# A two-layer graph network on one core: the transpose of h moved from TensorE to a DRAM scratch, block loads and VectorE, with the layer norm of x one stage earlier

## What is computed

```python
# layer 0
h = maximum(layernorm(x), 0)
q, k, v = h @ Wq.T + bq, h @ Wk.T + bk, h @ Wv.T + bv
weight = adj * exp(q @ k.T)
x = x + (weight / sum(weight, axis=2)) @ v
# layer 1
h = maximum(layernorm(x), 0)
A_hat = adj + eye;  d = A_hat.sum(-1) ** -0.5
x = x + (A_hat * d[:, :, None] * d[:, None, :]) @ (h @ W + b)
```

## Time and profile before

| | |
|---|---|
| three runs, us | 1748.71, 1750.32, 1751.24 (median 1750.32) |
| the profiled execution, us | 1750.99, its span 1749.1 |
| PE busy | 1725.3 us, 99% of the span |
| DVE, ACT, POOL busy | 1266.5, 746.5, 555.7 us |
| mean granted clock of TensorE | 0.997 of full speed |
| DMA moved | 105.55 MB, mean 60 GB/s |

### The profile page before, as it was taken

One profiled execution on the slowest core, in us unless ns is written; L12 is line 12 of the kernel. 1 busy time (PEld: TensorE's weight loads), 2 busy tenths in 40 slices (PEclk: granted clock), 3 DMA queues, 4 the chain that ended last, 5 costly groups with the idle time before them and its releaser, 6 DMA issues.

```text
span 1749.1 us, 32667 instructions
## 1 busy us (share of the span) xinstructions
PE 1725.3 (99%) x11452; PEld 1574.7 (90%) x11452; DVE 1266.5 (72%) x3097; ACT 746.5 (43%) x1546; POOL 555.7 (32%) x585
## 2 busy tenths in 40 slices
PE   7999999999999999999999999999999999999997
PEld 5899999999999999999999999999999999999996
DVE  5677777777777777777767777777777777777774
ACT  3444344353444444444443443534444444434432
POOL 1323323323323323333233233233233233332331
PEclk9999999999999999999999999999999999999999
DMA  5212212212122122122122121121221221221210
GB/s 157 61 43 66 69 39 72 60 48 72 54 54 72 54 54 72 48 60 71 41 68 67 41 72 55 53 72 54 54 72 51 57 72 43 65 69 39 72 48 25
DMA packets 191978, 105.55 MB, mean 60 GB/s; under 512 B 140512, under 2 KB 156896, under 8 KB 191968
## 3 DMA queue, kind: packets, MB, share of 16 engines
q1 hardware_dynamic: 190048, 103.84, 21.0%
q10 hardware_dynamic: 1920, 1.58, 0.3%
HBM read 71.83 MB, written 33.55 MB: 60 GB/s over the span
## 4 chain that ended last, share of the span: by engine, by line
PE 98%; DVE 1%; issue 0%; ACT 0%; DMA 0%; POOL 0%; ACTq 0%; POOLq 0%; DVEq 0%
PE ps L546 31%; PE ps L548 31%; PE ps L547 31%; PE ps L630 3%; PE ps L556 1%; PE ps L613 1%; DMA late<-in_L_gnn_Wq_w_dram 0%; ACT late L287 0%; DVE p_lo L515 0%; ACT h_hi L289 0%; DVE z_lo L486 0%; DVE late L492 0%; DVE w_in L395 0%; DVE wvt_lo L385 0%; POOL hat_lo L227 0%
## 5 line engine op out<-in xcount | busy, mean ns | idle before, releaser
L287 ACT ACTIVATE late<-late,nb,sc 128x512 f32<-128x512 f32 x128 | 103.6, 809 | 587.5 <-DVE nb L443 587.5
L546 PE MATMUL ps<-ht_hi,m_hi 128*128 128x256 f32 x1024 | 287.3, 281 | 0.8 <-DVE wvt_lo L385 0.8
L547 PE MATMUL ps<-ht_lo,m_hi 128*128 128x256 f32 x1024 | 288.0, 281 | 0.0
L548 PE MATMUL ps<-ht_hi,m_lo 128*128 128x256 f32 x1024 | 287.5, 281 | 0.0
L224 POOL TENSOR_TENSOR hat_hi<-adjt,eye 128x512 fp32r<-128x512 f32 x64 | 82.7, 1293 | 580.4 <-DVE p_lo L515 580.4
L546 PE MATMUL ps<-w_hi,z_hi 128*128 128x512 f32 x512 | 207.7, 406 | 1.5 <-DVE z_lo L486 1.5
L548 PE MATMUL ps<-w_hi,z_lo 128*128 128x512 f32 x512 | 202.4, 395 | 0.0
L547 PE MATMUL ps<-w_lo,z_hi 128*128 128x512 f32 x512 | 202.3, 395 | 0.0
L546 PE MATMUL ps<-wvt_hi,ht_hi 128*128 128x512 f32 x512 | 202.2, 395 | 0.0
L548 PE MATMUL ps<-wvt_hi,ht_lo 128*128 128x512 f32 x512 | 202.1, 395 | 0.0
L547 PE MATMUL ps<-wvt_lo,ht_hi 128*128 128x512 f32 x512 | 202.0, 395 | 0.0
(11 more groups left out here) (102 smaller groups left out, 4529.1 us busy)
## 6 DMA issues: line engine op xcount, KB each, us to landing
x_in<-in_x_dram SPq DMA_DIRECT2D x64, 512.0 KB, 3.5
out_dram<-late SPq DMA_DIRECT2D x128, 256.0 KB, 2.0
adj_in<-in_adj_dram SPq DMA_DIRECT2D x64, 256.0 KB, 2.8
adj_blocks<-in_adj_dram SPq DMA_DIRECT2D x256, 64.0 KB, 2.8
late<-in_L_gnn_Wk_w_dram SPq DMA_DIRECT2D x4, 256.0 KB, 4.9
late<-in_L_gnn_Wq_w_dram ACTq DMA_DIRECT2D x4, 256.0 KB, 7.7
wv_in<-in_L_gnn_Wv_w_dram SPq DMA_DIRECT2D x1, 1024.0 KB, 7.9
w_in<-in_L_gnn_W_dram SPq DMA_DIRECT2D x1, 1024.0 KB, 7.7
```

What stands on the lines that cost most here:

```text
L287: act.activation(h1[:, t, :], x1[:, t, :], ACT.Relu, scale=sc_1[:, t:t + 1], bias=nb_1[:, t:t + 1])
L546: pe.matmul(dst, a_hi[:, c, cols], b_hi[:, c, :], start=(c == 0), stop=False)
L547: pe.matmul(dst, a_hi[:, c, cols], b_lo[:, c, :], start=False, stop=False)
L548: last = pe.matmul(dst, a_lo[:, c, cols], b_hi[:, c, :], start=False, stop=(c == chunks - 1))
```

## The change

In all steps but the first, `h` is no longer transposed by PE. SP stores `h` to a DRAM scratch (`h_scratch`), waits for the store, and loads it back with four DMAs as 32x32 blocks (`load_h_blocks`); VectorE transposes the blocks with two instructions (`transpose_h`) to `ht` in SBUF; `ht_hi` and `ht_lo` are then made from `ht` where they were made from PSUM. So that `h` is there early enough, ScalarE makes `h` of the next graph as the first thing of a step instead of in the middle, and VectorE takes the statistics of x two graphs ahead. `x_in` is then free before the residual is needed, so x is loaded a second time, into `xb`, after `x1` of the graph before has been read, and GpSimd adds `bv` in place, later in its order. GpSimd also waits for `ht_lo` before it makes `hat`.

```diff
+        def load_h_blocks(sp):
+            rows = h_dram.rearrange("(g r) (c q j) -> q r c g j", r=32, c=DC, q=P // 32, j=32)
+            for q in range(P // 32):
+                sp.dma_start(h_blocks[q * 32:(q + 1) * 32].rearrange("r c (g j) -> r c g j", j=32),
+                             rows[q]).then_inc(h_blocks_loaded, 16)
...
             sp.dma_start(x_in[:], x[0].rearrange("(t p) d -> p t d", p=P)).then_inc(x_loaded, 16)
+            sp.dma_start(xb[:], x[0].rearrange("(t p) d -> p t d", p=P)).then_inc(xb_loaded, 16)
...
                     sp.dma_start(adj_in[:], adj_next.rearrange("(t p n) -> p t n", p=P, n=N)).then_inc(adj_loaded, 16)
+
+                    sp.wait_ge(h_ready[0], this + 1)
+                    sp.wait_ge(h_ready[1], this + 1)
+                    if prev:
+                        sp.wait_ge(h_blocks_loaded, (this - 1) * (16 * P // 32))
+                    sp.dma_start(h_dram.rearrange("(t p) d -> p t d", p=P), h[:]).then_inc(h_stored, 16)
+                if second:
+                    x_second = x_flat[bass.ds(sp.snap((this + 1) * (N * D)), N * D)]
...
+                    sp.dma_start(x_in[:], x_second.rearrange("(t p d) -> p t d", p=P, d=D)).then_inc(x_loaded, 16)
+                if main and prev:
...
+                    sp.wait_ge(x1_ready[0], this - 1)
+                    sp.wait_ge(x1_ready[1], this - 1)
+                    sp.dma_start(xb[:], x_this.rearrange("(t p d) -> p t d", p=P, d=D)).then_inc(xb_loaded, 16)
                 if main and ahead:
-                    sp.wait_ge(h_ready[1], this)
-                    sp.wait_ge(xb_ready, this)
-                    sp.dma_start(x_in[:], x_next.rearrange("(t p d) -> p t d", p=P, d=D)).then_inc(x_loaded, 16)
-                if main and ahead:
+                    sp.wait_ge(h_stored, this * 16)
+                    if prev:
+                        sp.wait_ge(ht_ready[1], this - 1)
+                    load_h_blocks(sp)
                     sp.wait_ge(adjt_ready, this)
                     load_blocks(sp, adj_next)
...
                     pool.wait_ge(p_lo_ready[1], this - 1)
+                    if main:
+                        pool.wait_ge(ht_lo_ready[1], this)
...
+                    pool.wait_ge(xb_loaded, this * 16)
+                    for t in range(NT):
+                        last = pool.tensor_tensor(xb[:, t, :], xb[:, t, :], bv_row[:], ALU.add)
+                    last.then_inc(xb_ready, 1)
...
+            def layer_norm_x(this, prev):
+
+                act.wait_ge(ln_x_ready, this + 1)
+                if prev:
+                    act.wait_ge(h_stored, (this - 1) * 16)
+                for t in range(NT):
+                    if prev:
+                        act.wait_ge(vk_ready[t], this)
+                    act.activation(h[:, t, :], x_in[:, t, :], ACT.Relu, scale=rs_x[:, t:t + 1],
+                                   bias=nb_x[:, t:t + 1]).then_inc(h_ready[t], 1)
...
+            def transpose_h(this, prev):
+
+                dve.wait_ge(h_blocks_loaded, this * (16 * P // 32))
+                for j in range(2):
+                    dve.wait_ge(ht_hi_ready[j], this)
+                    dve.wait_ge(ht_lo_ready[j], this)
+                    dve.transpose(ht[:, 2 * j:2 * j + 2, :].rearrange("p c n -> p (c n)"),
+                                  h_blocks[:, 2 * j:2 * j + 2, :].rearrange("p c n -> p (c n)")).then_inc(ht_ready[j], 1)
...
                     for c in range(DC):
-                        if prev and c % 2 == 0:
-                            pe.wait_ge(z_lo_ready[c // 2], this - 1)
                         for t in range(NT):
                             last = pe.transpose(ps[:, HT + c // 2, c % 2 * N + t * P:c % 2 * N + (t + 1) * P],
```

More of the change, by code:

```diff
@@ L162, in steps @@
             step(2, prev=True, main=True, ahead=True, older=False)
-            with eng.Fori(3, B) as this:
+            with eng.Fori(3, B - 1) as this:
                 step(this, prev=True, main=True, ahead=True)
-            step(B, prev=True, main=True, ahead=False)
-            step(B + 1, prev=True, main=False, ahead=False)
+            step(B - 1, prev=True, main=True, ahead=True, second=False)
+            step(B, prev=True, main=True, ahead=False, second=False)
+            step(B + 1, prev=True, main=False, ahead=False, second=False)
         @block.sync
@@ L215, in _, with step @@
             pool.wait_ge(ident_ready, 2)
-            def step(this, prev, main, ahead, older=True):
+            def step(this, prev, main, ahead, older=True, second=True):
                 if prev:
@@ L227, in step @@
                     pool.tensor_tensor(hat_lo[:], hat[:], hat_hi[:].bitcast(fp32), ALU.subtract).then_inc(hat_lo_ready, 1)
[L228 to L238, removed]
                     pool.wait_ge(ve_1_done, this - 1)
@@ L280, in value_high, with step @@
                 act.activation(v_hi[:, t, :, 0:HD], halves(ps[:, V + t, :]), ACT.Copy).then_inc(v_hi_ready[t], 1)
-            def step(this, prev, main, ahead, older=True):
+            def layer_norm_x(this, prev):
[7 more added lines that the diff above has]
+                                   bias=nb_x[:, t:t + 1]).then_inc(h_ready[t], 1)
+            def step(this, prev, main, ahead, older=True, second=True):
+                if main and ahead:
+                    layer_norm_x(this, prev)
                 if prev:
@@ L302, in step @@
                     value_high(1, this)
[L303 to L309, removed]
+                if ahead and not main:
+                    layer_norm_x(this, prev)
+                    m_high()
                 if prev:
@@ L458, in step @@
                         last.then_inc(g_lo_ready[j], 1)
[L459 to L479, removed]
+                if ahead and not main:
+                    statistics(this + 1)
+                    m_low()
+                if second and main:
+                    statistics(this + 2, lambda: value_low(0, this), lambda: value_low(1, this))
                 elif main:
@@ L482, in step @@
                     value_low(1, this)
+                if main and ahead:
+                    transpose_h(this, prev)
                 if prev:
@@ L527, in step @@
                         score_bias(this + 1)
+                        statistics(this + 2)
                 if prev:
@@ L576, in bias_and_wv_products, with step @@
                 pe.wait_ge(wvt_lo_ready, 2)
-            def step(this, prev, main, ahead, older=True):
+            def step(this, prev, main, ahead, older=True, second=True):
                 if main:
+                    pe.wait_ge(ht_lo_ready[0], this)
                     pe.wait_ge(ht_lo_ready[1], this)
@@ L619, in step @@
                                 (g_hi, g_lo), cols, (ht_hi, ht_lo)).then_inc(s_done[t], 1)
[L620 to L623, removed]
+                if ahead and not main:
+                    m_product()
+                    pe.wait_ge(ident_ready, 1)
                     pe.wait_ge(h_ready[0], this + 1)
```

59 lines of the change are left out of this document (47 added, 12 removed).

## The result

The changed kernel takes 1703.34 us (median of 4, 1702.79 to 1703.71) against 1750.65 us for the kernel before beside it (4 runs, 1748.71 to 1751.24). The ratio is 0.9731, 95% interval 0.9715 to 0.9748. Predicted were 1704, faster, in 1697 to 1735. The profiled execution took 1703.36 us, span 1701.6.

The account below looks back on a forecast made before the run. PE was taken as the bound, busy for all 26.58 us of a step. 1751.0 - 54.6 (transposes) + 8.0 (start-up) = 1704.4 us, 1703.7 for the median; forecast 1704, own range 1700 to 1708, stated range 1697 to 1735.

Parts of the forecast that it names:

- 0.88 us a step for the transposes on PE: Between S and O1 on PE, removing eight transposes saves 0.88 us in each of 62 steps, 54.6 us.
- DVE's 1.42 us are hidden: Two block transposes on DVE between nb_x and z_lo fit its idle time; z_lo keeps 1.0 to 1.6 us before O1.
- The start-up, +8 (4.9 to 9.9): In step 1, O waits for h's store, loads and transposes ahead of p, beginning 4.9 to 9.9 us later; 8 taken.
- Block loads land 10.6 us after G starts (8.1 to 13.1): Last block load of h lands at 911.0 to 916.0, middle 913.5, before DVE's turn at 915.8; PE loses nothing.
- Rival 1: Blocks of h land late, DVE stands ahead of z_lo, kernel slower; landing at 919.5 gives 1834 us; 11%.
- Rival 2, POOL and DVE block each other: POOL's xb add falls beside DVE's h_lo; held by one add 1704 to 1720 us, by both 1760; 16%.
- `hat` behind `ht_lo`: nothing: POOL's hat starts 1.2 us later, takes 3 x 1.3 us, needed by Z 11.3 us after G starts: no cost.
- DMA share 0.45: The DMA engines' share of a step rises from 0.20 to some 0.45, as 1.5 MB a step become 3.
- Layer norm ahead: ACT makes the next graph's h at the step's start; the forecast sum counts no gain for this.

Follow-up runs that it names:

- experiment 1: Changed kernel with PE's eight transposes of h put back between S and O1, their result read by nobody: 1757.94 us, 1.0043 of the kernel before.
- experiment 8: Changed kernel with DVE, in step 1 alone, making graph 3's statistics and the transposes of h behind p_lo: 1697.31 us, 0.9706 of the kernel before.
- Experiment 7: Changed kernel in which POOL's hat no longer waits for ht_lo: 1711.79 us (median of three), 0.9776 of the kernel before.
- experiment 2: Changed kernel with only the earlier layer norm and second x load; PE transposes h as before, no scratch or block loads: 1753.95 us, 1.0022 of the kernel before.
- experiments 9 to 11: POOL makes rs_x ahead of the xb add, added to the kernels with two more DVE transposes, four more, and hat not waiting for ht_lo: 1711.87, 1784.45, 1709.92 us.
- experiment 4: Changed kernel with four more DVE block transposes behind the wait for the block loads, from step 2 on: 1797.49 us, 1.0269 of the kernel before.

## Why the prediction was right, point by point

The forecast was 1704.4 for the profiled execution, which took 1703.36. The loop gave 54.1 us where 54.6 were foretold, and the start-up cost 6.8 where 8 was taken out of a range of 5 us. That the sum came within 1.1 us is the mechanism for the loop, and in part luck for the start-up.

- *0.88 us a step for the transposes on PE*: 0.35 us between the two starts as foretold; the step went from 26.57 to 25.70, 0.87. Shown by experiment 1, which puts it back.
- *DVE's 1.42 us are hidden*: 1.30 us, hidden; 1.57 us remain to O1 in the step shown (1.0 to 1.6 foretold). But the prediction priced this slack in one undisturbed step. `nb_x` is up to 1.49 us late in others, and what is left there is 0.2 us. That no step of the loop lost time was closer than the working knew, and so partly luck.
- *The start-up, +8 (4.9 to 9.9)*: 6.8. O begins at 54.97, inside 53.1 to 58.1. It is due to DVE's order, since experiment 8 takes it away. By the terms, `h` stood at 40.2 (39.4 foretold), the store landed at 43.4 (42.9), the last block at 49.9 (47.9 to 52.9). The working left out that the statistics of the third x stand ahead of the transposes and wait 2.48 us for their load; they were done at 48.4, ahead of the blocks.
- *Block loads land 10.6 us after G starts (8.1 to 13.1)*: too early. In steps 3 to 62 of after the last one lands at 12.25 in the median, from 10.7 to 14.0. The store lands at 3.8 (3.1 foretold); from the first issue to the last it is 4.9 us (2.2 to 4.4 foretold), and that term is the one that was mis-sized; from the last issue to the landing 3.6 (2.8 to 5.6). DVE's turn is at 12.8, and by the slack of 1.69 PE loses from some 14.5 on. For the loads of x the 3.5 us of the earlier trace rows did not hold either: each step sends 1.5 MB more through the same queue, and they land in 6.6 and 7.6 us. Rival 1 was nearer than its 11% looked: two more loads cost some 38 us, 1741.21 against 1703.34.
- *Rival 2, POOL and DVE block each other*: happened, at another instruction than the one named, and inside the slack. `h_lo` has 727 ns in the mean and is held in 3 cases of 122 between 80 and 1650 us, up to 1.78 us. The `xb` add was expected at 908 to 913, 5 to 10 us behind G; it comes at 9.0 in the median, when DVE is past `h_lo` (7.2 us) and close to `ve_x` (11.7). It holds `ve_x` in 17 of 60 steps. What the prediction hadn't named at all is POOL's own order: `rs_x` waits behind `xb`, in those steps too, and in 5 more that the order alone makes late, the worst of them.
- *`hat` behind `ht_lo`: nothing*: right as made. Experiment 7 shows what the wait avoids, some 8 us.
- *DMA share 0.45*: 0.51.
- *Layer norm ahead*: right that it brings nothing by itself (experiment 2).

Why the loads scatter in their landing isn't settled: in steps 3 to 62 of after `xb` is issued 1.4 to 2.0 us behind G and lands 6.9 to 10.9 behind it, and no run here separated the queue from the memory. That the losses left in experiments 9 to 11 are mostly the block loads' is read from the waits, and no run took it away.

## What to carry to other kernels

When one engine has no idle time in the loop, take whole instructions off it and price them by the distance between starts with and without them; the receiving engine needs slack at that place in its chain, not in its total. Read that slack in the worst step, not in one: list what stands in the same in-order queues behind a transfer (here `rs_x` behind the add of a load) and what runs beside it on the engine that shares SBUF with it (here `ve_x`), and add traffic to a queue at the price of its later landings. In the first step nothing is hidden, so the order of the engines there wants a look of its own.

## What the runs showed of the hardware

- A DVE and a POOL instruction that both read SBUF slowed each other. `ht_lo` (two SBUF inputs) went from 687 to 1238 ns beside `hat_hi`, and `hat_hi` from 1291 to 1537. The Trainium skill, "SBUF — State Buffer", section "Who interferes with whom", says that such a DVE instruction contends with a GpSimd one that reads SBUF; the trace agrees, and shows a loss on both sides.
- An instruction of DVE that reads one tile was held too: `ve_x`, 0.17 us alone, took up to 1.27 us beside POOL's add on `xb`, and in 17 of 60 steps of after it ended 0.02 to 0.03 us behind an add.
- After some waits PE ran at half clock (1.2 instead of 2.4 GHz). Behind the 9.17 us in step 1 the granted clock is 0.50 from 54.97 to 56.90 and the matmuls of O follow at 0.21 us, later at 0.12. In a step of experiment 4 (G at 195.81) PE had waited 1.91 us. Its O1 begins at 215.11, and from 216.1 to 219.5 the matmuls follow at 0.43 us instead of 0.23. Windows of that step, the next, and that stretch:

```profile
195.81:225.20 29.39, 27.48 (x173) 24.71 (x171) 23.32 (x54) 11.73 (x24) 10.04 (x11) 0.94 0.48 116
225.20:251.67 26.47, 25.96 (x172) 23.61 (x171) 22.85 (x54) 11.74 (x24) 7.20 (x9) 1.00 0.44 109
...
216.10:219.50 3.40, 3.40 (x9) 2.61 (x8) 3.22 (x13) 1.72 (x5) 0.00 (x0) 0.50 0.00 0
```

  The granted clock of that step is 0.94 and the next one's 1.00, and the step is 29.39 us where its late `nb_x` alone gives 27.85. Seven such steps, behind waits of 1.90 to 3.04 us, are most of the rest of that experiment's loss: there a late delivery to PE cost its wait and 1.5 to 3.0 us more. Three other waits of that run, of 2.11 to 2.47 us, were followed by no half clock.
- How long SP took to issue four loads with runs of 128 bytes (512 KB) went with what else was under way: 2.75 us in step 1, 3.28 to 7.50 in the loop. The adjacency's four (256 KB) took 3.06.
